# A Mamba block with routed experts: decays moved to SBUF, two-tile scans, PSUM banks for the experts, narrower zeroing, a new order

## The reference

```
h = x + mamba(layernorm(x));  m = gelu(layernorm(h) @ w1.T + b1) @ w2.T + b2
x = layernorm(x + h + m)
mamba:  xc, z = split(xn @ in_proj.T);  xc = silu(conv4(xc) + conv_b)
        dt, B, C = split(xc @ x_proj.T);  dt = softplus(dt @ dt_proj.T + dt_b)
        h[t] = exp(dt[t] * A) * h[t-1] + dt[t] * x[t] * B[t];  y[t] = C[t] . h[t]     (16 states)
        out = ((y + xc * D) * silu(z)) @ out_proj.T
experts: scores = softmax(x @ gate.T); the best 2 of 8 for each token, weighted, plus one shared expert
x = layernorm(x + experts(x))
```

## Time and profile before

| | |
|---|---|
| median of three runs | 6628.13 us |
| profiled execution, its own time | 6627.49 us |
| its span in the trace | 6625.8 us |
| mean granted TensorE clock | 0.791 |
| PE busy | 4812.6 us (73%) |
| DVE busy | 4681.8 us (71%) |
| POOL busy | 3583.6 us (54%) |
| ACT busy | 3140.8 us (47%) |
| DMA moved | 596.96 MB, mean 90 GB/s |

### The profile page before, as it was taken

How to read it: one execution, slowest core, us unless ns; L and a number is a source line. 1 busy time by engine, 2 the same in 40 slices (tenths; PEclk the granted TensorE clock), 3 DMA queues, 4 the chain that set the end, 5 groups by cost and what they waited for, 6 DMA issues and landing times. The chain is left out here.

```text
span 6625.8 us, 75794 instructions
## 1 busy us (share of the span) xinstructions
PE 4812.6 (73%) x20928; PEld 3400.8 (51%) x20928; DVE 4681.8 (71%) x7114; ACT 3140.8 (47%) x5026; POOL 3583.6 (54%) x2319
## 2 busy tenths in 40 slices
PE   2577777777777776777777677787777787777764
PEld 0355545555555555555555555555555555555553
DVE  1877777777677777777777777777777777777721
ACT  2444445445455454555545455544545554454421
POOL 1555555555444566664456666445666646665523
PEclk8577777777788887788877788887778888877886
DMA  8743111122111223331122332212243323432445
GB/s 258 225 177 132 31 36 38 39 77 76 58 60 52 64 86 96 94 79 61 52 64 84 97 93 78 62 52 66 80 112 91 83 70 106 118 107 69 113 115 153
DMA packets 361842, 596.96 MB, mean 90 GB/s; under 512 B 36545, under 2 KB 184130, under 8 KB 361298
## 3 DMA queue, kind: packets, MB, share of 16 engines
q1 hardware_dynamic: 236690, 382.01, 19.0%
q10 hardware_dynamic: 75584, 142.83, 6.3%
q0 software_dynamic: 49152, 67.27, 5.0%
HBM read 372.47 MB, written 219.50 MB: 89 GB/s over the span
## 5 line engine op out<-in xcount | busy, mean ns | idle before, releaser
L459 POOL TENSOR_TENSOR dBx<-dtx,Bbc 128x1024 f32<-128x1024 f32 x1024 | 2414.7, 2380 | 1355.1 <-DVE hs L1024 1074.5
L1024 DVE TENSOR_TENSOR_SCAN hs<-ps,dBx 128x512 f32<-128x512 f32 x2048 | 2414.4, 1207 | 214.4 <-ACT ps L609 126.2
L790 PE MATMUL ps<-ident,hs 128*128 128x128 f32 x8192 | 1587.4, 345 | 1060.2 <-DVE acc L1040 602.5
L790 PEld LDWEIGHTS ps<-ident,hs 128*128 128x128 f32 x8192 | 1244.0, 179 | 1572.1 <-DVE acc L1040 771.4
L609 ACT ACTIVATE ps<-dt,A 128x512 f32<-128x512 f32 x2048 | 1393.3, 688 | 1120.5 <-DVE hs L1024 1068.1
L1040 DVE SCALAR_TENSOR_TENSOR acc<-ps,C_tok,acc 128x512 f32<-128x512 f32 x1792 | 1288.4, 736 | 353.2 <-PE ps L790 331.1
L950 PE MATMUL ps<-post_tmp,wx 128*128 128x128 f32 x2560 | 457.2, 352 | 100.9 <-issue 100.2
L511 POOL DMA_INDIRECT fx<-Y_slots,slots x256 | 401.0, 1567 | 219.4 <-DMA fx<-shared 98.9
L950 PEld LDWEIGHTS ps<-post_tmp,wx 128*128 128x128 f32 x2560 | 426.2, 260 | 144.0 <-issue 143.5
L493 POOL DMA_INDIRECT X_slots<-xs,slots x256 | 256.4, 1002 | 346.6 <-ACT dt L594 290.8
L1009 DVE SCALAR_TENSOR_TENSOR xc<-ps,conv_w,xc 128x511 f32<-128x511 f32 (+2 forms) x384 | 285.6, 744 | 191.3 <-ACT xc L569 184.4
(11 more groups left out here) (164 smaller groups left out, 6336.9 us busy)
## 6 DMA issues: line engine op xcount, KB each, us to landing
Bbc<-B_scratch SPq DMA_DIRECT2D x512, 256.0 KB
wx<-in_experts SPq DMA_DIRECT2D x320, 384.0 KB
X_slots<-xin ACTq DMA_DIRECT2D x26, 2056.0 KB, 21.4
Y_slots<-xin ACTq DMA_DIRECT2D x26, 2048.0 KB, 13.2
xin<-X_slots SPq DMA_DIRECT2D x320, 128.5 KB
...
```

Source lines behind the costliest of these rows:

```text
L459: pool.tensor_tensor(dBx[u % 3][:], dtx[b % 2][:, 2 * h:2 * h + 2, :], Bbc[g % NBB][:, n % CH:n % CH + 1, :].broadcast_to([P, 2, T]), ALU. ...
L790: i = pe.transpose(psH[w % 2][:, j * P:(j + 1) * P], hs[(n * CT + j) % NHB][:, t * P:(t + 1) * P], ident[:])
L1024: dve.tensor_tensor_scan(hs[s % NHB][:], psA[s % 2][:], dBx[s // 2 % 3][:, s % 2, :], 0.0, ALU.mult, ALU.add).then_inc(s_scan, 1)
```

## The change

- The decays go to SBUF: `dA`, two buffers of two tiles each, so that ACT may be four tiles ahead instead of two. The first column of the second tile is zero, so that one scan of 1024 columns does two tiles (32 scans for a batch, into five buffers of two tiles). Both tensor operands of the scan now lie in SBUF.
- The two banks that were `psA` become `psE`, for the experts alone, with `xsT` and `ge` as SBUF buffers of their own (one each, where there were two). The result overwrites `xin`, and SP waits for its store before it loads the next rows there. `opens` and the waits between `post` and the experts go.
- `OPENED` is `(0,)`: ACT opens one sum for a batch; DVE weighs 60 pieces instead of 56; PE turns half as many sums at the end.
- `X_slots` is no longer cleared. Its last rows get zeros at the start, and before a group's first pair SP writes 128 zero rows behind each expert's last row (8 DMAs, positions in `ends`) and waits for them. `Y_slots` is cleared by 228 DMAs of 256 KB from a DRAM block of zeros, spread over the first 12 batches.
- `PERIODS` is `NB + 3`, up to 12 pairs and, near the end, 3 finishes in a period. The last two groups use rows of their own and don't wait for the gathers of the group two before.
- Small tables share one SBUF tensor `few`; the shared expert's residual is transposed back from `mT`; `AT` is new throughout.

```diff
-    NHB = 9
-    OPENED, NACC = (0, NS // 2), 3
+    NHP, NDA = 5, 2
+    OPENED, NACC = (0,), 2
-    PERIODS, PAIRS_MAX, FINS_MAX = NB + 8, 8, 2
+    PERIODS, PAIRS_MAX = NB + 3, 12
-        fins_in[b] = list(range(finished, min(ready, finished + FINS_MAX)))
+        fins_in[b] = list(range(finished, min(ready, finished + (2 if b < NB - 6 else 3))))
...
-    "DVE_scan": [-2.42, -2.42, 4.13, 4.13, 4.19, 4.35, 5.02, 5.02, 5.02, 5.22, 5.51, 8.41, 10.2, 10.2, 12.09, 12.09,
+    "DVE_scan": [0.51, 3.74, 3.74, 3.74, 7.45, 7.71, 8.33, 10.11, 10.73, 13.84, 15.58, 17.09, 19.69, 23.61, 26.42,
...
# ACT, scan()
-                    if s >= 2:
-                        act.wait_ge(s_scan, s - 1)
+                    if s // 2 >= NDA:
+                        act.wait_ge(s_scan, s // 2 - NDA + 1)
-                    act.activation(psA[s % 2][:], dt[b % 2][:, j, :], ACT.Exp, scale=A[:, j, n:n + 1]).then_inc(s_dA, 1)
+                    act.activation(dA[s // 2 % NDA][:, j % 2, j % 2:], dt[b % 2][:, j, j % 2:], ACT.Exp,
+                                   scale=A[:, j, n:n + 1]).then_inc(s_dA, 1)
...
# DVE, scan()
-                    dve.tensor_tensor_scan(hs[s % NHB][:], psA[s % 2][:], dBx[s // 2 % 3][:, s % 2, :], 0.0,
-                                           ALU.mult, ALU.add).then_inc(s_scan, 1)
+                    dve.tensor_tensor_scan(*[v[:].rearrange("p a t -> p (a t)") for v in (
+                        hs[u % NHP], dA[u % NDA], dBx[u % 3])], 0.0, ALU.mult, ALU.add).then_inc(s_scan, 1)
...
# ACT, clear()
-                for i, rows in enumerate((X_slots[0], X_slots[1], Y_slots[0], Y_slots[1])):
...
+                act.dma_start(zeros, nothing).then_inc(s_zeros, 16)
+                for i in range(2):
+                    act.dma_start(X_slots[i][NE * ROOM:ROWS, :].rearrange("(p a) d -> p a d", p=P), nothing[:, 0:ROW].rearrange(
+                        "p (o d) -> p o d", o=1).broadcast_to([P, (ROWS - NE * ROOM) // P, ROW])).then_inc(s_behind, 16)
+                for i in range(2):
+                    rows = Y_slots[i].rearrange("(p n a) d -> p n (a d)", p=P, a=2)
+                    for k in range(CLEARS):
+                        yield first[i] + groups[i] * k // CLEARS
+                        if (i, k) == (0, 0):
+                            act.wait_ge(s_zeros, 16)
+                        act.dma_start(rows[:, k, :], zeros[:, 0:2 * D]).then_inc(s_Y_cleared[i], 16)
...
# SP, experts()
+                            for e in range(NE):
+                                r = sp.value_load(ends[g % 2][0:1, e:e + 1], min_val=0, max_val=ROWS - P)
+                                sp.dma_start(X_slots[g % 2][bass.ds(r, P), :], zeros[:, 0:ROW]).then_inc(s_padded[g % 2], 16)
+                            sp.wait_ge(s_padded[g % 2], (g // 2 + 1) * NE * 16)
                         if p >= 2:
-                            sp.wait_ge(s_yo, (p - 1) * 2)
+                            sp.wait_ge(s_Y_out[k], stores(p - 2, k))
...
# PE, inputs() and results()
-                        if opens(b, p):
-                            pe.wait_ge(s_hidden_s, per_batch(b, 0, 2))
                         if p:
-                            pe.wait_ge(s_xsT, p)
+                            pe.wait_ge(s_yo, p * 2)
-                                i = pe.transpose(psG[0][:, (m * KD + k) * P:(m * KD + k + 1) * P],
+                                i = pe.transpose(psE[0][:, (m * KD + k) * P:(m * KD + k + 1) * P],
...
-                        if opens(b, p):
-                            pe.wait_ge(s_sum, (b + 1) * 2)
...
-                            i = pe.matmul(psY[:, m * D:(m + 1) * D], ge[p % 2][:, m * P:(m + 1) * P],
+                            i = pe.matmul(psE[0][:, m * D:(m + 1) * D], ge[:, m * P:(m + 1) * P],
```

More of the change, by code:

```diff
@@ L141, in build @@
     CAP = max(groups) * T
-    ROWS = NE * CAP + 16 * P
+    ROOM = CAP + P
+    ROWS = NE * ROOM + 28 * P
     NKEPT = 16
+    OFF = [groups[g - 2] * T + P if g >= NG - 2 else 0 for g in range(NG)]
+    before = [g - 4 if g >= NG - 2 else g - 2 for g in range(NG)]
     pairs_to = [sum(tiles[:g + 1]) // 2 for g in range(NG)]
-    PERIODS, PAIRS_MAX, FINS_MAX = NB + 8, 8, 2
+    PERIODS, PAIRS_MAX = NB + 3, 12
     pairs_in, fins_in = [[] for _ in range(PERIODS)], [[] for _ in range(PERIODS)]
@@ L219, in build @@
         slots = sb("slots", [P, NKEPT, 2, NTB], mybir.dt.uint32)
-        cap8, count = sb("cap8", [P, NE]), sb("count", [P, NE])
-        full, tile_no = sb("full", [1, NE, CAP // P]), sb("tile_no", [1, NT])
-        fills, cum0, cum1 = [sb(f"m8_{i}", [1, NE]) for i in range(3)]
-        beyond = sb("beyond", [1, NT, NE])
-        over = beyond[:].rearrange("p i e -> p (i e)")[:, 0:NE * (CAP // P)].rearrange("p (e n) -> p e n", e=NE)
-        at_row, at_expert = sb("at_row", [1, NT]), sb("at_expert", [1, NT])
-        where = [sb(f"where{i}", [1, 2, NT], mybir.dt.int32) for i in range(2)]
+        count, bases = sb("count", [P, NE]), {o: sb(f"base{o}", [P, NE]) for o in sorted(set(OFF))}
+        few = sb("few", [P, DI + T])
+        M0, B2 = 64, 96
+        w_dt, dbc = few[0:R, 0:DI], few[0:NX, DI:DI + T]
+        b2 = few[B2:B2 + 1, 0:D]
+        taken, table = 0, []
+        for n in (NE * (CAP // P), NT, NE, NE, NE, NT * NE, NT, NT):
+            table.append(few[M0:M0 + 1, taken:taken + n])
+            taken += n
+        full, tile_no, fills, cum0, cum1, beyond, at_row, at_expert = table
+        over = beyond[:, 0:NE * (CAP // P)].rearrange("p (e n) -> p e n", e=NE)
+        full, beyond = full.rearrange("p (e n) -> p e n", e=NE), beyond.rearrange("p (i e) -> p i e", e=NE)
+        where = [sb(f"where{i}", [P, 2, NT], mybir.dt.int32)[M0:M0 + 1, :, :] for i in range(2)]
+        ends = [sb(f"ends{i}", [P, NE], mybir.dt.int32)[M0:M0 + 1, :] for i in range(2)]
+        xsT, ge = sb("xsT", [P, T]), sb("ge", [P, HALF])
         xin = [sb(f"xin{i}", [P, 2, ROW]) for i in range(2)]
@@ L231, in build @@
         ps = [ctx.enter_context(nc.psum_tensor(f"ps{i}", [P, 512], F32)) for i in range(8)]
-        psA, psH, psP, psY, psG = ps[0:2], ps[2:4], ps[4], ps[5], ps[6:8]
+        psE, psH, psP, psY, psG = ps[0:2], ps[2:4], ps[4], ps[5], ps[6:8]
         B_scratch = nc.dram_tensor("B_scratch", (NB, NS * T), F32, kind="Internal").ap()
@@ L249, in build @@
         s_x_in = [sem(f"x_in{i}") for i in range(NX_IN)]
-        s_cleared = [sem(f"cleared_{n}") for n in ("X0", "X1", "Y0", "Y1")]
+        s_Y_cleared, s_zeros, s_behind = [sem(f"Y_cleared{i}") for i in range(2)], sem("zeros"), sem("behind")
+        s_padded = [sem(f"padded{i}") for i in range(2)]
         s_kept, s_stored = sem("kept"), sem("stored")
@@ L649, in post @@
                         act.wait_ge(s_m_turned, per_batch(b, k, KD))
-                        if k == 0 and b and pairs_in[b - 1]:
-                            for i in range(2):
-                                act.wait_ge(s_Y_out[i], stores(pairs_in[b - 1][-1], i))
                         act.activation(mT[:, k, :], psG[k][:], ACT.Identity, scale=norm2[:, 0, k:k + 1],
@@ L937, in experts @@
                     for p in pairs_in[b]:
[L938 removed]
+                        w = wx[p % 2]
                         for m in range(2):
@@ L974, in _ @@
         def _(dve):
+            dve.memset(where[0], 0).then_inc(s_consts, 1)
+            dve.memset(where[1], 0).then_inc(s_consts, 1)
+            for k in range(CAP // P):
+                dve.memset(full[:, :, k:k + 1], float(k * P)).then_inc(s_consts, 1)
+            for k in range(NT):
+                dve.memset(tile_no[:, k:k + 1], float(k)).then_inc(s_consts, 1)
             dve.wait_ge(s_weights, ALL_WEIGHTS)
```

257 lines of the change are left out of this document (121 added, 136 removed), and 25 rows, old and new, of the table AT.

## The result

The changed kernel takes 6788.1 us in the median against 6630.0 for the kernel before: 1.0232 of its time, with a 95% interval of 1.0212 to 1.0252. It is slower where I forecast 6530 us and faster. Rival 2, the exclusion paid in the open, had 6778. The changed kernel's four executions took 6784.65, 6791.49, 6780.1 and 7110.84 us, and the last, with a granted TensorE clock of 0.669 against 0.81 in the others, is in the median but not in the ratio. The profiled execution took 6784.65 us, its span is 6782.9.

The account below looks back on a forecast made before the run. No engine was full; the lists of DVE, PE and ACT interlocked, with DVE setting the pace. From 6627.5: start -40, small clears +10, tail -95, periods without experts +51, with experts -24, giving 6530 us; range 6300 to 6840.

Parts of the forecast that it names:

- Rival 2: DVE's scans against POOL's products: exclusion paid in the open, 16 us a period instead of 8, 6778 us; chance 0.26.
- The scan's second SBUF operand: DVE scans and POOL products exclude one another once decays lie in SBUF: +8 us a period, ends 0 and 33.
- the 33 that I had as the far end: Upper end for the exclusion of scans and products: every gap and every product pays, 24.5 + 8.6 us a period.
- the six gaps without other work: Six of 32 gaps between DVE's scans hold no other work; products ready ahead, so no cost.
- 7 of the 11.4: Eleven gaps between DVE's scans lack 11.4 us of other work; with DVE idle 39% outside scans, 7 us counted.
- Decays and the new order: DVE's waits for decays vanish with four tiles ahead: -2 us a period without experts, -3.5 with; no term for the order.
- Scans and weighings: On DVE: a 1024-column scan takes 2.17 us, 1.6 less a batch; four more weighings cost 2.9; together +1.3 us.
- Experts apart: Batches with experts, now 13.6 us a period dearer, save half of that with their own banks: -6.8 us.
- Start: Before the first scan: fewer clears ahead of the first norm, blocked 20 to 43 us instead of 72, saving 40 us.
- Tail: After the last scan: 236 us instead of 338, 95 taken off, ends 40 and 120; over 300 would make it wrong.

Follow-up runs that it names:

- experiment 3: Products computing 16 of 512 columns: kernel before 6553.7 us, kernel before with decays in SBUF 6711.6, changed kernel 5930.4; with full products 6636, 7598.1, 6788.1.
- small products: Each POOL product for dBx computes only 16 of 512 columns of its tiles; 5930.4 us in the changed kernel, 6553.7 in the kernel before.
- experiment 2: Kernel before with only its decays moved to SBUF, two buffers of one tile, scans still 512 columns: 7598.1 us, ratio 1.1453.
- The two stages: Separate small kernel, 584 us in all: SBUF scans beside POOL products, one stage with scans of 1024 columns (107.4 us for 24), one with 512.
- experiment 7: Kernel before with the change's clears alone: 6682.5 us. With no clears ahead of the first norm: kernel before 6562.1 us, changed kernel 6753.5.

## Why the prediction was wrong, point by point

**The scan's second SBUF operand** is the step that failed. That scans and products exclude one another was right, the size was not. I took +8 us a period, 248 in all; experiment 3 gives 776, which is 25 a period, and the hold itself is 30 us a batch, close to the 33 that I had as the far end. The step reads "32 x 4.3 + 4 x 2.15 = 146 us, within 181 and 194.5: it needn't lengthen anything". Three things were wrong in it. I gave the six gaps without other work no cost, because the next scan would be queued before POOL hears of a free buffer; but three scans in a row take 12.95 us, with a product to each, so such a gap pays in full. "DVE is idle for 43 of 110 us anyway, 39%, so I count 7 of the 11.4" took idle time as cover: DVE's idle time in a batch without experts is 17 us with small products and 18 with full ones, so it covered nothing. And the sum held only the products: POOL's gathers, scatters and norm steps are one queue with them, which makes it 167 to 210 us and not 146. That sum alone would not have told the loss either, since only with three finishes does it pass the old period (210 against 208). The end that I left out of the range, 33 us a period, is what the part costs by itself (963 / 31 = 31, experiment 2, of which the 886 us that small products take away are 29). The signs were there: scan mean 3.20 against the 2.25 that was to show it, POOL's product 2.95 against 2.38. With experts the period is 200.4, above the 200 that I had given as rival 2's sign.
The rule of the Trainium skill on this ("SBUF — State Buffer", "Who interferes with whom") holds here in its main point, a lock and no sharing of bandwidth: 107.4 = 52.5 + 55.2 us. It says that issue order decides who blocks. The two stages fit it: POOL was first where a scan waited for 57.2 us, DVE where they took turns, though the width differed too.

**Decays and the new order** are the step that was missing. I gave the decays -2 and -3.5 us and the tables nothing at all. DVE's waits for the decays did shrink from 6.4 to nothing in the window 741:1290 and from 83.3 to 7.7 us in 1560:6100, but waits for products took their place (178 us in all; before, the 46.2 of `issue`, which end with a product too, and 25.2 make 71). But the rest of the change is worth 623 us when the products are small. In the two traces 18 come from the start, 43 from the tail, and 555 from between first and last scan (6051.2 to 5496.5 us). My forecast had -98 - 248 = -346 for all of it, -211 of them between first and last scan. The two errors have opposite signs, 528 and 277 us; that the time came out inside the range owes to this. Rival 2 was right that the exclusion is paid in the open; that its 6778 lies 10 us from the measured time is luck, since it had 16 us a period for the one and nothing for the other.

**Scans and weighings.** 2.17 was forecast for a scan of 1024 columns, 2.19 is the distance of two when alone (52.45 / 24). Right. The errata rule of the Trainium skill ("VectorE: DVE Perf Modes"), which would have made SBUF scans cheaper, isn't borne out: 24 scans of 512 columns take 26.9 us from SBUF and 26.8 from PSUM.

**Experts apart.** -6.8 a period was taken. It can't be read alone: the batches with experts and no finish came out 0.7 us shorter than before.

**Start.** -19.5 instead of -40. Below are the timeline rows that answer to the earlier trace rows. ACT is blocked for 43.4 us, not 20: the last transfer lands at 69.4 us, so 10 us of work were still in the queue when ACT went on, and I had counted 20. That is the far end of my 20 to 43, where I took 32. The 72 us of before were too many as well: with no clear ahead of the norm its first scan starts 61 us earlier (experiment 7). In the changed kernel the same move brings the first scan 37 us forward.

```profile
15.98 0.35 ACTq L550 DMA_DIRECT2D zeros<-xin  x1
16.38 9.81 ACTq L552 DMA_DIRECT2D X_slots<-xin  x2
26.22 33.11 ACTq L560 DMA_DIRECT2D Y_slots<-zeros  x19
59.38 2.07 ACT L571 ACTIVATE dtx<-xt,nb_pre,rs_pre 128x256 f32<-128x256 f32 x4 [45.63 <-issue]
...
125.94 4.32 DVE L1030 TENSOR_TENSOR_SCAN hs<-dA,dBx 128x1024 f32<-128x1024 f32 x1 [11.85 <-ACT dA L625]
```

**Tail.** -37 instead of -95. PE's and SP's rows of it, for the earlier trace rows:

```profile
6482.18 2.28 DVE L1030 TENSOR_TENSOR_SCAN hs<-dA,dBx 128x1024 f32<-128x1024 f32 x1
...
6500.18 1.11 PE L937 MATMUL ps<-ident,xin 128*128 128x128 f32 x4 [6.68 <-DMA xin<-X_slots]
6509.32 0.97 PE L937 MATMUL ps<-ident,xin 128*128 128x128 f32 x4 [1.02 <-ACT xin L721]
6521.30 1.12 PE L937 MATMUL ps<-ident,xin 128*128 128x128 f32 x4 [3.07 <-DMA xin<-X_slots]
...
6647.41 9.91 SPq L376 DMA_DIRECT2D X_slots<-zeros  x8
...
6666.40 1.11 PE L937 MATMUL ps<-ident,xin 128*128 128x128 f32 x4 [28.30 <-DMA xin<-X_slots]
```

The last batch's `post`, with eight pairs between its steps, ends at 6638, 156 us behind the last scan; I had 82 + 20. A pair there takes some 10 us. PE waits before it in turn for ACT to write the result of the pair before (1.02 us) and for rows that SP loads only behind the store of an earlier result (3.07 us at 6521). What follows takes 145 us, where I had 8 + 116 + 10 = 134. The group's zero rows fall into it: PE is idle for 28.3 us around them, 9 of these before the first of the eight is sent. I had 8 for them, and none at all in the batches, where experiment 7 finds 10 to 17 us for a group. The tail is 300.7 us, just over the 300 that I had named as the sign that the term is wrong.
